# First layer's bias moved into the experts' weights, and the weights made during the recurrence

## What is computed

```python
x = x + L0_gnn(layernorm(x), adj)     # five small graph convolutions over the first 25 nodes
x = x + L0_ffn(layernorm(x))          # LSTM-like recurrence over 256 steps, batch 32, hidden 128
x = x + L1_gnn(layernorm(x), adj)     # normalised adjacency, 256 nodes, then a linear map W, b
x = x + L1_ffn(layernorm(x))          # router and experts:

xn = (x - mu) * rsqrt(var + eps) * gamma + beta
logits = xn @ Wr + br;  the two largest of 8, softmax over them
for e in range(8):
    h = gelu(xn @ W1[e] + b1[e])      # 128 -> 256
    y += (h @ W2[e] + b2[e]) * weight[e]
```

## Time and profile before

| | us |
|---|---|
| median of 3 runs | 918.02 (916.75 to 922.01) |
| profiled execution | 922.89 |
| its span | 921.1 |
| PE, DVE, ACT, POOL busy in the span | 753.2, 620.6, 433.5, 303.3 |
| recurrence, 256 steps | about 88 to 548 |
| second graph block and router | about 548 to 700 |
| expert pages | about 700 to 904 |

### The profile page before, as it was taken

One profiled execution on the slowest core, in us unless ns is written; L12 is line 12 of the kernel. 1 busy time (PEld: TensorE's weight loads), 2 busy tenths in 40 slices (PEclk: granted clock), 3 DMA queues, 4 the chain that ended last, 5 costly groups with the idle time before them and its releaser, 6 DMA issues.

```text
span 921.1 us, 23562 instructions
## 1 busy us (share of the span) xinstructions
PE 753.2 (82%) x7636; PEld 505.2 (55%) x7636; DVE 620.6 (67%) x3020; ACT 433.5 (47%) x1584; POOL 303.3 (33%) x472
## 2 busy tenths in 40 slices
PE   0995998888888888888888889768628999999994
PEld 0873555545445444454544547656515777777773
DVE  6334777777777777777777764777743776667673
ACT  1123554454444544444444433435514676766662
POOL 5600121322222122221111112475761444444443
PEclk9995555555555555555555559779758999999997
DMA  5990111111110111101111025364222323332320
GB/s 141 177 292 1 36 42 41 30 41 34 40 40 29 40 34 40 40 28 40 34 40 40 28 73 174 104 202 133 77 87 69 85 81 87 85 85 83 87 75 4
DMA packets 78795, 66.71 MB, mean 72 GB/s; under 512 B 8633, under 2 KB 75456, under 8 KB 78704
## 3 DMA queue, kind: packets, MB, share of 16 engines
q1 hardware_dynamic: 71103, 52.65, 21.2%
q0 software_dynamic: 5984, 12.74, 4.0%
q10 hardware_dynamic: 1642, 0.49, 0.2%
HBM read 40.28 MB, written 27.32 MB: 73 GB/s over the span
## 4 chain that ended last, share of the span: by engine, by line
PE 50%; DVE 23%; ACT 16%; issue 8%; POOL 0%; DMA 0%; another core or an unknown queue 0%; DVEq 0%; SPq 0%; POOLq 0%; ACTq 0%
PE pb L799 10%; DVE pb L1437 7%; ACT tanh_c L1110 5%; DVE h L1439 5%; ACT GC L1106 4%; PE pb L866 3%; PE pb L1001 3%; PE pb L996 3%; PE pb L1016 3%; ACT S L1108 3%; PE pb L836 3%; PE pb L1003 2%; PE pb L1002 2%; PE pb L1018 2%; PE pb L1017 2%
## 5 line engine op out<-in xcount | busy, mean ns | idle before, releaser
L799 PEld LDWEIGHTS pb<-h,vp 128*128 128x128 bf16 x3840 | 142.3, 106 | 191.0 <-DVE h L1439 187.0
L799 PE MATMUL pb<-h,vp 128*128 128x32 f16 x3840 | 171.8, 190 | 54.8 <-DVE h L1439 42.6
L679 POOL DMA_INDIRECT out<-outb,out_i x91 | 91.1, 1001 | 128.5 <-DVE outb L1627 118.1
L770 PE MATMUL pb<-xbuf,us 128*128 128x256 f32 x198 | 118.2, 703 | 0.0
L1106 ACT ACTIVATE GC<-pb 128x32 f32<-128x32 f32 x256 | 51.7, 202 | 139.8 <-PE pb L799 139.8
L1615 DVE SCALAR_TENSOR_TENSOR glo<-Gl,pw,ghi 128x512 f16<-128x512 f32 x91 | 68.4, 752 | 63.9 <-ACT ghi L1227 63.9
L1437 DVE TENSOR_TENSOR_SCAN pb<-S,GC 128x64 f32<-128x64 f32 x256 | 77.5, 303 | 39.9 <-ACT S L1108 26.7
L1110 ACT ACTIVATE tanh_c<-pb 128x32 f32<-128x32 f32 x256 | 50.7, 198 | 94.8 <-DVE pb L1437 94.8
L1439 DVE SCALAR_TENSOR_TENSOR h<-S,tanh_c 128x32 f16<-128x32 f32 x256 | 49.2, 192 | 67.8 <-ACT tanh_c L1110 67.8
L1221 ACT ACTIVATE Gl<-pb,pw 128x512 f32<-128x512 f32 x91 | 62.7, 689 | 60.3 <-PE pb L1003 57.7
L667 POOL DMA_INDIRECT xs_d<-stg,slot x64 | 63.3, 990 | 45.5 <-DVE slot L1540 28.3
(11 more groups left out here) (324 smaller groups left out, 1685.2 us busy)
## 6 DMA issues: line engine op xcount, KB each, us to landing
Xp<-xs_d SPq DMA_DIRECT2D x91, 130.0 KB
adjn<-in_adj SPq DMA_DIRECT2D x32, 256.0 KB, 2.7
x_d<-x2s SPq DMA_DIRECT2D x33, 128.0 KB, 1.8
y_d<-ys SPq DMA_DIRECT2D x33, 128.0 KB, 1.8
X<-in_x SPq DMA_DIRECT2D x4, 912.0 KB, 16.4
xs_d<-zrow SPq DMA_DIRECT2D x1, 3640.0 KB, 13.1
yr<-y_d SPq DMA_DIRECT2D x8, 256.0 KB
x2r<-x_d SPq DMA_DIRECT2D x8, 256.0 KB
```

Of the source, the lines that this page charges most:

```text
L679: pool.indirect_dma_start(out_rows, bass.IndirectOffsetOnAxis(out_i[t % 4][:, 0:1], 0), outb[t % 4][:], None, bounds_check=B * T - 1, oob_ ...
L770: mm(o, us[:, q, :], xbuf[:], start=False, stop=False, skip_group_check=True)
L799: return mm(o, vp[p][:, q, :], h[:], start=False, stop=True, skip_group_check=True)
```

## The change

The first layer's bias no longer has a matmul of its own. A normalised row sums to zero, so one of its 128 entries is redundant: W1 is replaced by `fold`-multiplied weights, whose rows 0 to 126 are the differences to row 127 (times gamma), and row 127 holds beta times W1 plus b1. The last row of xT is a constant, set once by POOL.

- 16 `bias_piece` matmuls (48 output rows) become 16 `fold_piece` matmuls (128 output rows) at other steps; ACT copies them back over W1 in four copies of 512 columns. The squares move. The matmul that sums `folded` moves from step 5 to step 7 of tile 3.
- POOL adds b1 to the last row in tiles 10 to 13 (eight adds on 32 partitions by 256 columns) and makes parts of b2 alone, 128 columns wide. Four small instructions are added to `powers_0`, two scalings and a product removed.
- The weights are made in tiles 16 to 31 of the recurrence, from the copies already on chip: one ACT scaling of two experts at once (256 columns) in step 3, one DVE split at the end of step 7. ACT and DVE have separate loops of two tiles for it; PE's loop is unchanged.
- The loads of `wq` and all splits in the router stage go. y and x2 have separate semaphores and are loaded as y, y, x2, x2.
- In a page L996 and its `sel1` address are gone; L1215 and L1609 write 127 rows.

```diff
+        def expert_pair(second, c, pair):
+            two = bass.ds(pair * 2, 2)
+            parts = [w[c][k][:].rearrange("p (e n) -> p e n", n=P)[:, two, :] for k in range(2) for w in ((w2,) if second else (w1,))]
+            return (w2st[:, two, c, :], tau2) if second else (wst[:, two, c * P:(c + 1) * P], tau1), parts
 # SP
-            for f in range(2, NB2):
+            def load_y(f):
                 if f >= NLD:
                     sp.wait_ge(ht_ps, f - NLD + 1)
+                sp.dma_start(yr[f % NLD][:], y_nodes[:, :, bass.ds(f * (2 * D), 2 * D)]).then_inc(y_loaded[f % NLD], 16)
+
+            def load_x2(f):
+                if f >= NLD:
                     sp.wait_ge(x3_ready, f - NLD + 1)
-                load(f, f % NLD)
-                if f >= 3 and f % 2:
-                    load_expert(f // 2 - 1)
-            load_expert(E - 1)
+                sp.dma_start(x2r[f % NLD][:], x2_nodes[:, :, bass.ds(f * (2 * D), 2 * D)]).then_inc(x2_loaded[f % NLD], 16)
 # POOL
+                if part < 4:
+                    if part == 0:
+                        pool.wait_ge(ld_bias, 16 * 8)
+                    pool.wait_ge(folded_w, part + 1)
                     for j in range(2):
-                        cols = slice(j * P, (j + 1) * P)
+                        last = wst[P - 32:, 2 * part + j, :]
                         behind_h2(5 + j)
-                        link(pw(bb[:, cols], bb[:, cols], other[:, cols], op))
+                        pw(last, last, b1row[P - 32:, (2 * part + j) * HID:(2 * part + j + 1) * HID], ALU.add).then_inc(biased, 1)
+                        pool.wait_ge(biased, 2 * part + j + 1)
+            pool.wait_ge(y_loaded[0], loads(0))
+            for x in xT:
+                tp.memset(x[:, 0:P], SC)
+                tp.memset(x[:, P:], 0.0)
 # PE
+            def fold_piece(n):
+                if n % 4 == 0 and n:
+                    pe.wait_ge(folded_w, n // 4)
+                m = mm(beta_b[:, (n % 4) * P:(n % 4 + 1) * P], fold[:], wst[:, n // 2, (n % 2) * P:(n % 2 + 1) * P],
+                       start=(n % 4 == 0), stop=True, skip_group_check=True)
-BIAS_STEPS = [(0, 1, 6, 7)] * 3 + [(0, 1)]
+FOLD_STEPS = [(0, 1, 2, 3, 6, 7)] + [(0, 1, 6, 7)] * 2 + [(0, 1)]
-                        if once and q4 == 3 and s in (0, 1):
-                            bias_piece(13 + 2 * s)
-                        if once and q4 == 3 and s == 5:
-                            pe.wait_ge(bsum_ready, 1)
+                        if once and q4 == 3 and s == 7:
+                            pe.wait_ge(folded_w, 4)
                             pe.wait_ge(folded_ready, 1)
-                mm(h[:].rearrange("p (i n) -> p i n", n=P), b1T[:], bc(sel1[:, bass.ds(vs, 4)].unsqueeze(2), [NK, 4, P]),
-                   start=True, stop=False, skip_group_check=True)
 # ACT
+            def split_upper(second, c, pair):
+                (src, by), (hi, _) = expert_pair(second, c, pair)
+                av(hi, src, ACT.Copy, scale=by).then_inc(whi_ready, 1)
+            groups(0, 4, once=True)
+            with act.Fori(1, NGRP // 8) as it:
+                groups(it, 4)
+            act.wait_ge(powers_ready, 1)
+            act.wait_ge(biased, E)
+            for second in range(2):
+                with act.Fori(NGRP // 4 + second * NGRP // 8, 3 * NGRP // 8 + second * NGRP // 8) as it:
+                    groups(it, 2, split=second)
 # DVE
+            def split_lower(second, c, pair, G):
+                (src, by), (hi, lo) = expert_pair(second, c, pair)
+                dve.wait_ge(whi_ready, G + (1 - NGRP // 2))
+                v.scalar_tensor_tensor(out=lo, in0=src, scalar=by, in1=hi, op0=ALU.mult, op1=ALU.subtract).then_inc(wlo_ready, 1)
+                        if split is not None and s == STEPS - 1:
+                            split_lower(split, q4, it - (NGRP // 4 + split * NGRP // 8), G)
-                split_lower(F, 0)
                 assign(F)
-                split_lower(F, 1)
```

More of the change, by code:

```diff
@@ L195, in build @@
             w2st = sb("w2st", [P, E, 2, D], where=pre)
-            squared = sb("squared", [P, 512], where=pre)
-            betak = sb("betak", [P, 16 * (NK + 1)], where=pre)
+            fold = sb("fold", [P, P], where=pre)
+            b1row = sb("b1row", [P, E * HID], where=pre)
             zrow = sb("zrow", [P, ROW], where=pre)
@@ L609, in biases @@
+                if part == 7:
                     pool.wait_ge(ld_kons, 16)
                     link(ts(bb[:], bp[0][:], m3(0), None, ALU.mult))
[L611 to L617, removed]
+                if part in (8, 9):
+                    link(ts(bbr[:], bp[part - 7][:], m3(part - 7), None, ALU.mult))
+                    behind_h2(5)
+                    link(pw(bb[:], bb[:], bbr[:], ALU.add))
@@ L858, in aggregate @@
                 u = f % 2
[L859 to L862, removed]
+                pe.wait_ge(y_loaded[f % NLD], loads(f))
+                if f >= 2:
                     pe.wait_ge(hts_ready, f - 1)
@@ L1000, in layer1 @@
                         o = h[:, (2 * j + c) * P:(2 * j + c + 1) * P]
-                        mm(o, w1[c][0][:, bass.ds(v, P)], x[:, 0:P], start=False, stop=False, skip_group_check=True)
+                        mm(o, w1[c][0][:, bass.ds(v, P)], x[:, 0:P], start=(j == 0 and c == 0), stop=False, skip_group_check=True)
                         mm(o, w1[c][0][:, bass.ds(v, P)], x[:, P:], start=False, stop=False, skip_group_check=True)
@@ L1140, in four_groups @@
-                        if once and q4 == 3 and s == 4:
-                            act.wait_ge(beta_ps, 1)
-                            av(bsum[:], beta_b[0:NK, 0:P], ACT.Copy).then_inc(bsum_ready, 1)
+                        if split is not None and s == 3:
+                            split_upper(split, q4, it - (NGRP // 4 + split * NGRP // 8))
+                        if once and s == 3 + (q4 == 0):
+                            act.wait_ge(fold_ps, q4 + 1)
+                            av(flat[0][:, 512 * q4:512 * q4 + 512], beta_b[:], ACT.Copy).then_inc(folded_w, 1)
@@ new lines, in groups @@
+                        if once and (q4, s) in SQUARES:
+                            j = SQUARES.index((q4, s))
+                            if j == 0:
+                                act.wait_ge(ld_w, 48)
+                            av(squared, flat[j // 4][:, 512 * (j % 4):512 * (j % 4) + 512], ACT.Square,
+                               accum_out=sq[:, j // 4, j % 4:j % 4 + 1]).then_inc(squares_ready, 1)
+                        if once and (q4, s) == (3, 2):
+                            act.wait_ge(prep_ready, 1)
+                            act.wait_ge(ld_bias, 16 * 8)
+                            av(squared[0:2 * E, 0:P], b1s[:], ACT.Square, accum_out=folded[0:2 * E, 3:4]).then_inc(squares_ready, 1)
@@ L1427, in fill, with groups @@
                     ins.then_inc(x_aggr, 1)
-            with dve.Fori(0, NGRP // 4) as it:
-                for q4 in range(4):
-                    G, k = it * 4 + q4, q4 % 2
+            def split_lower(second, c, pair, G):
+                (src, by), (hi, lo) = expert_pair(second, c, pair)
+                dve.wait_ge(whi_ready, G + (1 - NGRP // 2))
+                v.scalar_tensor_tensor(out=lo, in0=src, scalar=by, in1=hi, op0=ALU.mult, op1=ALU.subtract).then_inc(wlo_ready, 1)
+            def groups(it, n, split=None):
+                for q4 in range(n):
+                    G, k = it * n + q4, q4 % 2
                     for s in range(STEPS):
-                        t = it * (4 * STEPS) + (q4 * STEPS + s)
+                        t = it * (n * STEPS) + (q4 * STEPS + s)
                         cols = slice(s * B, (s + 1) * B)
@@ L1444, in _ @@
                         fill(G, k, s, it)
+                        if split is not None and s == STEPS - 1:
+                            split_lower(split, q4, it - (NGRP // 4 + split * NGRP // 8), G)
+            with dve.Fori(0, NGRP // 8) as it:
+                groups(it, 4)
+            for second in range(2):
+                with dve.Fori(NGRP // 4 + second * NGRP // 8, 3 * NGRP // 8 + second * NGRP // 8) as it:
+                    groups(it, 2, second)
             dve.wait_ge(hT_ps, NGRP + 1)
@@ L1466, in residual @@
                     dve.wait_ge(rows_sent[F % NBUF], 16 * NT * (F // NBUF))
-                dve.wait_ge(cd_loaded[f % NLD], loads(f))
+                dve.wait_ge(x2_loaded[f % NLD], loads(f))
                 dve.wait_ge(c_ps, f + 1)
```

193 lines of the change are left out of this document (72 added, 121 removed).

## The result

| | us | ratio to the kernel before, 95% interval |
|---|---|---|
| kernel before, first pair | 918.37, median of 4 | |
| changed kernel, first pair | 890.61 (886.65 to 894.08), median of 4 | 0.9666 [0.9618, 0.9715] |
| kernel before, second pair | 905.74, median of 9 | |
| changed kernel, second pair | 877.76 (876.52 to 878.46), median of 5 | 0.9691 [0.9674, 0.9707] |

The forecast was 892.4 with a range of 883 to 900. On each of them the kernel before took 905.0 to 905.8 us, 13 less than in the first pair, so the changed kernel was measured again on one of them, together with the kernel before: the second pair. The profiled execution of the changed kernel in the first pair took 889.91 us, its span is 888.1.

A forecast was written before the change was run, and what follows sets the result against it. TensorE was taken to bound the pages, with a two-page ring of TensorE, ACT and DVE next. Terms -21.1 - 5.3 - 0.5 + 0.5 + 0.8 = -25.6 us gave 892.4 us from the median of 918.02, range 883 to 900.

The forecast's parts named there:

- Pages: Expert pages: 91 bias matmuls and one address per page go, a page takes 2.01 instead of 2.20 us, -21.1 us.
- The ring of two pages: Expert pages: TensorE, ACT and DVE wait on each other over two pages, 4.01 to 4.02 us, becoming the bound.
- the offset waits: Expert pages: every fourth page loads TensorE's offsets, 0.21 us more; within the two-page limit this costs nothing more.
- Routing: Stage before the pages: ACT and DVE lose the weight-making instructions, so slots come sooner, -5.3 us, bounds 0 to -9.
- Recurrence: Recurrence: -0.5 us for the first 32 steps, +0.5 for POOL's adds, +0.8 for the splitting.
- The pieces added in steps 2 and 3: Recurrence, first tile: two pieces delay step 3 by about 0.45 us and step 2 by 0.15.
- POOL's adds: Recurrence, tiles 10 to 13: eight 256-column adds cost 0.2 to 0.25 us each, +0.5 net, bounds -1 and +5.
- the sixteen splits: Recurrence, end of step 7: DVE splits cost 0.05 us each, +0.8 us, bounds 0 and +4.
- A: Rival, expert pages: TensorE still sets the page at 1.88 us, -29 instead of -21.1, 884.4 us; chance 0.10.
- B: Rival, routing: gives nothing, taken up by stalls or TensorE's lower clock level, 897.7 us; chance 0.17.
- C: Rival, expert pages: idle TensorE drops to 1.2 GHz, slower from 17 such pages, 952 us at 40; chance 0.04.
- D: Rival, recurrence: pays for addresses and the port, +7 instead of +0.8 us, 898.6 us; chance 0.07.

The follow-up runs named there:

- the first experiment: Changed kernel with DVE making the lower half of xT of page t+2 before the combine of page t-2: 863.11 us, ratio 0.9537.
- the doubled splits: Changed kernel with a second DVE split of the same size behind each of the sixteen in the recurrence: 882.74 us.
- the lengthened ring: Changed kernel with one more DVE instruction (128x128 sum into an unused tile) at the end of each page's combination: 886.94 us.

## Why the prediction was right, step by step

**Pages, -21.1 forecast (-20.8 from first to last page), -22.2 and -22.4 measured from first to last.** The ring of two pages held to the hundredth: 4.02 us against 4.01 to 4.02, with the hand-over of 0.06 us. The forecast's 3.37 for the filling and 88 times 2.01 make 180.3, which is what the second pair shows. The 2.5 us for single late pages was too much; one page cost 1.3 in the first pair, none in the second. That the offset waits would vanish in the ring was right: there are 21, of 4.3 us in all, and pairs stay at 4.02. Wrong was a detail: TensorE's own page is 1.78, not 1.88. The start-to-start distance of L996, 0.32 us, was not all that it held: the gap from the transpose to layer 1 fell from 0.21 to 0.12 us too. So of 0.42 us freed, the ring gave back half. I also expected a wait for xT in nearly every page; there is one in every second, since the ring only fixes pairs.

**Routing, -5.3 forecast, -9.9 and -3.3 measured.** The mechanism (slots come sooner because splits leave ACT and DVE) is shown by the run with the splits put back. The size was off in both pairs, too small in one and too large in the other, and this is the mis-sized term. I took the stall pattern of one execution, 7.84 us at tile 3, as a property of the kernel. In the kernel before with its pages reordered, tile 3 doesn't wait for slots at all. In the changed kernel that wait is 2.86 us in the first pair (I had said some 6.5) and 0.81 in the second. Of the bounds, 0 and -9, the lower was passed by 0.9.

**Recurrence, +0.8 forecast, -0.6 measured in both pairs.** The sign of this term was wrong. The two doubled steps went, as forecast, and so did the three longer ones: the first 32 steps take 57.0 us instead of 58.5. The pieces added in steps 2 and 3 cost nothing instead of 0.6, but the clock has a part in it. Two microseconds of the changed kernel, first pair:

```profile
90.00:92.00 2.00, 1.44 (x21) 0.93 (x20) 1.62 (x10) 1.17 (x7) 0.00 (x0) 1.00 0.00 0
```

and the same two of the kernel before:

```profile
90.00:92.00 2.00, 2.00 (x21) 1.11 (x20) 1.55 (x9) 1.04 (x7) 0.00 (x0) 0.50 0.00 0
```

TensorE ran there at 2.4 GHz, and I had reckoned with the earlier trace rows, at 1.2. In the first experiment, where the clock was 0.50 from 92 to 94 us, step 3 took 1.87 us: 0.09 more than a plain step, and not 0.45. POOL's adds were forecast at +0.5 and cost 0.9 us (steps 80 to 176 take 173.7 us in the first pair, 172.8 before); the sixteen splits were forecast at +0.8, and the steps that they end take 1.78, for the reason that the doubled splits showed. One step of 2.08 us (step 128, the first of the new loops of two tiles) was not forecast: the prediction had put those loops at nothing. Its cause wasn't looked for. Steps 128 to 255 together take 227.1 us, 227.2 before.

The Trainium skill (SBUF — State Buffer, "Who interferes with whom") says of VectorE's modes with two ports that whichever of GpSimd and VectorE issues first has the shared ports for its whole instruction, and the other fully blocks, and it names tensor_scalar among the instructions that can enter them. The rows of L1416 agree with it in that the order decides: 0.82 us behind the add, 0.35 ahead of it. They agree with a block too, since DVE's instruction ends by the add's end and not by its own start: the scaling ended 0.15 us behind the first add (241.36 against 241.21), and the scan at 243.10 ended 0.16 us behind the second (243.45 against 243.29). POOL's own delay in the other order isn't shown as clearly: its add took 0.80 us behind the scaling, and 0.77 ahead of it. What I had made of the rule was too wide in one way, eight adds that each hold up a whole instruction (four did), and too narrow in another: I had weighed it by a scan, not by the instruction that stood beside the add.

**Rivals.** A (TensorE sets the page) is excluded by the lengthened ring; it became true only with the new order, and then 41.9 us under the kernel before instead of the 33.6 of A's 884.4, since TensorE's page was shorter than I had read. B (routing gives nothing) is excluded in both pairs, though the second's 3.3 us are 2.0 short of the forecast. C (the clock falls) didn't come: 1.00 throughout the pages, although TensorE idled 0.28 us before every fourth page, less before the late page between, and 1.63 us once, before the layer 1 at 692.92. It did fall after a stop of 3.7 us. The Trainium skill (TensorE: Matmul & The Clock Gate, "A second HAM failure mode: psum-queue depth-cycling") tells of a clock that swings with short idles between groups of matmuls; no run here shows that for the idles of up to 1.63 us in the pages. D (the recurrence pays 7 us) is excluded: from the first scan to the last it took 457.3 us, 0.6 less than before.

**The sum.** Forecast -25.6; measured -27.8 in the first pair (918.4 to 890.6) and -28.0 in the second. The second's parts: pages -22.4, routing -3.3, recurrence -0.6, together -26.3 of the two spans' 26.2 (the medians differ by more, since the trace of the changed kernel is of its slowest execution and the other is from another chip). The two profiled executions of the first pair differ by 33.0, and that of the kernel before lay 4.5 over its median of four; up to 5 of the 9.9 us of its routing may be just that. That the total came within 2.4 us is in part luck: in the second pair the pages gave 1.6 and the recurrence 1.4 more than forecast, and routing 2.0 less.

## What to carry to other kernels

When the engine that bounds a loop gets shorter, look at once for the ring over two turns behind it: add start-to-start distances from the first instruction through the other engines back to the same one two turns later, and ask which instruction of it nobody in the ring needs. Here it was a combination of 0.64 us that no engine of the ring waits for; moving it cost nothing and gave half as much again as the change. Such a move can't be judged on the kernel before: there it was worth 0.0 us.

A stall read in one execution is a sample: compare waits over two executions, and over two chips where there are two, before a term of several us is built on one.

## What I had not expected of the hardware

- An instruction of 0.28 us on DVE moved the next start by 0.20, one of 0.46 by 0.37 to 0.40. Rows' durations on DVE overlap, as PE's do; starts add up.
- DVE's 256-column fp32 tensor_scalar took 0.82 us behind a POOL instruction of 0.77 that had started 0.10 us earlier, and 0.35 when it started 0.13 us ahead of one.
- Taking away a 48-row matmul with 0.32 us to the next start freed 0.42 us.
- Loading 12 offsets into TensorE's registers held it for 0.2 us; loading 18 held it for 3.6 to 3.9 us every second time and 0.9 the others, and behind the first stop of 3.7 us the clock fell to 0.50.
- The kernel before took 918 us in the first pair and 905.0 to 905.8 on four chips later. In the traces (921.1 against 902.9 us, the latter with its pages reordered) 15.6 of the difference lie in the router's stage (154.4 against 138.8 us), with stalls by "remote" in the first alone. Whether this belongs to the chip or to the time of the runs wasn't tried.
